# Routing of a mixture of experts: an eight-highest search, shares in one step, a weight load in six pieces

## The chip, the cores and the metric

The kernel runs on one core of a Trainium2 chip. The metric is the device time of one execution in microseconds (us); lower is better.

## The reference

`x` is 32 sequences of 128 tokens with 128 features. Four blocks follow one another, each added to `x` and each behind a LayerNorm: a 16-head cross attention to a context of 77 tokens followed by a self attention and a feed-forward part; a mixture of 8 experts with two experts per token and a shared expert beside them; a two-way cross attention with a gate; a mixture in which each expert picks its 33 tokens of a sequence. The change lies in the second block:

```python
xn = xf * rsqrt(mean(xf * xf) + eps)                # xf: 4096 tokens
probs = softmax(xn @ router_w.T)                    # 8 experts
topk_p, topk_i = top_k(probs, 2)                    # ties: the lower expert first
rw = topk_p / sum(topk_p)                           # the two shares of a token
# the first 640 tokens of each expert, in token order, are dispatched
eout = (silu(xg @ rg) * (xg @ ru)) @ rd             # routed experts
shared = (silu(x @ sg) * (x @ su)) @ sd             # shared expert
return shared + routed
```

## The kernel before

**Tiling.** The 32 sequences are 8 groups of `GB` = 4. Tokens of a sequence lie on the 128 partitions. Attention is worked off in 16 units (`UNITS`): the cross attention (`c`) and self attention (`s`) of each group; self attention of groups 0 to 7 is unit 4, 6, 8, 10, 12, 13, 14, 15 (`SPOS`).

**Order.** Every engine runs the same loop over beats `n` from -11 to 159, written out by hand in `sp`, `pe`, `dve`, `act` and `pool`. Unit `i` starts at beat `8 i`; a step is placed by `d = n - 8 i`. Within a beat each engine has a fixed order of its steps and waits on semaphores. So a late step of one engine holds what is queued behind it there. The score maxima of a unit, eight beats of PE matmuls (L603), DVE reductions (L1196), ACT exponentials (L1665) and value products (L636), are the fabric. From beat 118 on the shared expert's matmuls (`shared`, L781, L782, L790) are woven in: 2, then 7/3 of them a beat. Each passes from PE to ACT (tanh, L1720) to DVE (L1350, L1354), and PE may take a bank again when DVE is done with it. Behind the loop the routed experts run, then the third and fourth blocks.

**Routing, on DVE**, for the group `g` of a self attention unit:
- `logits` (`d` = 30, L1260) writes eight logits for each of the 4 sequences.
- `choose` (`d` = 31, last in its beat but for LayerNorms). It compares every logit with every other (256 elements per token), adds a tie rule, sums to a rank, and takes rank 0 and rank 1 as `RR`. `SEL` is their sum; the scan L1293 makes the running count along the group and raises `v_sel`.
- `margin` (`d` = 32, L1300 to L1307): the difference of the two logits, `DEN`. ACT takes its exponential at `d` = 33 (L1794).
- `cum` on PE (`d` = 35 for groups 0 to 2, 33 for the others, L769, L770) waits for `v_sel` and sums over the tokens.
- `counts` and `places` (one and two beats behind `cum`) give the place of each token. POOL writes the tokens out with them (`scatter`, L2027).
- `shares` (`d` = 41 for groups 0 to 3, 37 for the others, L1335 to L1342): `w0 = 1 / (1 + DEN)`, `w1 = DEN w0`, and zero where the place is over capacity. `combine` reads them long after, in the third block.

**Spreads and loads, on SP.** In beats `d` = -16 to -12 of a unit SP spreads its queries and keys over partitions (`spread_k` L443, `spread_q` L447, a mask L436 or L438). PE's scores of that unit start at `d` = -11 and wait for all of them. At `d` = -1 SP sends the row of maxima (L489). The shared expert's weights `Wc`, 128 rows of 12 KB, are one load at beat 40 (L533), behind the first keys of unit 7:

```python
if n == 40:
    e.dma_start(Wc, A["pc"][:, 0:3072]).then_inc(d_wc, 16)
```

PE needs them from beat 118 on.

Of the kernel before, what the change touches and what calls it, by code (L numbers as in the profile page):

```python
# [9 lines left out]
I32 = mybir.dt.int32  # L10
U32 = mybir.dt.uint32
ALU = mybir.AluOpType
# [11 lines left out]
C_ID, C_LT, C_AT, C_IO, C_TR, C_EB, C_EC, C_MK, C_N = 0, 128, 256, 384, 417, 481, 489, 497, 537  # L24


def constants():
# [12 lines left out]
    c[:, C_TR:C_TR + 64] = (np.arange(8)[None, :] < np.arange(8)[:, None]).reshape(-1)  # L40
# [157 lines left out]
def program(nc, A, out, cst):  # L198
    ctx = ExitStack()
    with ctx:  # L200
# [61 lines left out]
        RR, RP, M2, IDF = r(128, 2, GB, 8), r(128, 2, GB, 8), r(128, 2, GB), r(128, 2, GB)  # L262
        DEN = r(128, GB)
        CMP, CM2 = r(128, GB, 8, 8), r(128, GB, 8, 8)
# [149 lines left out]
        def sp(e):  # L414
# [69 lines left out]
            for n in range(BEAT0, BEAT1):  # L484
# [47 lines left out]
                if n == 40:  # L532
                    e.dma_start(Wc, A["pc"][:, 0:3072]).then_inc(d_wc, 16)  # L533
# [53 lines left out]
        def pe(e):  # L587
# [186 lines left out]
            def shared(k):  # L774
                (hw, c), B = SHSEQ[k], bank_of(k)
                if c < 8:
                    xt = XLT[:, 256 * hw:256 * hw + 256]
                    L.wait_ge(a_t2, hw // 2 + 1)
                    L.wait_ge(d_wc, 16)
# [360 lines left out]
        def dve(e):  # L1140
# [128 lines left out]
            def choose(g):  # L1269

                Lg = grp(LG, g)
                other = Lg.unsqueeze(2).to_broadcast([128, GB, 8, 8])
                own = Lg.unsqueeze(3).to_broadcast([128, GB, 8, 8])
                tri = CST[:, C_TR:C_TR + 64].unsqueeze(1).to_broadcast([128, GB, 64])
                c1, c2 = (a.rearrange("p b e f -> p b (e f)") for a in (CMP, CM2))
# [20 lines left out]
            def margin(g):  # L1296

                R, P = rr()
# [19 lines left out]
            def places(g):  # L1318
# [5 lines left out]
                L.tick(e.tensor_reduce(IDF, RP, AX, ALU.add))  # L1324
                L.own_done()
                e.tensor_copy(IDX.bitcast(I32)[:, :, gb], IDF).then_inc(v_idx, 1)
                L.tick(e.tensor_scalar(M2, IDF, float(E1 * CAP1), None, ALU.min))
# [3 lines left out]
            def shares(g):  # L1331
                gb = slice(GB * g, GB * g + GB)
                w0, w1_ = WT[:, 0, gb], WT[:, 1, gb]
                L.wait_ge(a_ex, g + 1)
# [7 lines left out]
                L.tick(e.tensor_tensor(WT[:, :, gb], WT[:, :, gb], IDF, ALU.mult))  # L1342
# [17 lines left out]
            for n in range(BEAT0, BEAT1):  # L1360
# [142 lines left out]
            def r_top(u):  # L1503
                sm, sco = SM[u % 2], SCO[u]
                smb = sm.unsqueeze(2).to_broadcast([128, 8, 8])
                L.wait_ge(a_ex, NG + u + 1)
# [670 lines left out]
```

## Time and profile before

| | us |
|---|---|
| three runs | 1137.52, 1141.02 (median), 1141.60 |
| profiled execution, its own time | 1140.32 |
| its span in the profile | 1138.5 |
| PE busy | 989.6 |
| DVE busy | 676.0 |
| ACT busy | 590.1 |
| POOL busy | 468.6 |
| mean granted clock of PE | 0.928 of full |

How to read it: the span is what the trace covers, 1.8 us less than the execution's own time. PE's matmuls are pipelined, so its busy time overstates it somewhat. Busy times are averages over stages: the attention stage lies from 0 to about 440 us, attention's end together with the shared expert to 614, the routed experts to about 730, the last two blocks behind. A row of the timeline reads: start, duration, engine, line, operation, tiles and shapes, count, and in square brackets the idle time of the engine ahead of it with what ended it. A tile called `arena` is any of many in one large buffer. `issue` stands where nothing that the profile shows was waited for.

### The profile page before, as it was taken

To read this page: it belongs to the slowest core of one execution; us is meant where nothing else is said; L and a number is where in the kernel's file an instruction comes from. 1 tells how busy PE (TensorE), PEld (TensorE's weight loads), DVE (VectorE), ACT (ScalarE), POOL (GpSimd) and SP (SyncE) were. 2 spreads that over 40 slices of the span, in tenths; PEclk is the share of its full clock that TensorE was granted. 3 is DMA by queue.
4 is the path that set the end of the run, shared out by engine and by line. 5 is a ranking of instruction groups with operands and counts; after the bars stand their busy time and mean duration, and the time that the engine had idled before them with its cause. 6 is when DMAs were issued, how large, how long until landed. Compare 5 with 4: busy or idle time off the path is not lost.

```text
span 1138.5 us, 23362 instructions
## 1 busy us (share of the span) xinstructions
PE 989.6 (87%) x8694; PEld 771.1 (68%) x8694; DVE 676.0 (59%) x2162; ACT 590.1 (52%) x1350; POOL 468.6 (41%) x752
## 2 busy tenths in 40 slices
PE   4888888797888878978998999988887897898998
PEld 2666555566565656767787888766776686787877
DVE  4556664767676777557684333366788458366241
ACT  4667668686766767633333333223432644645553
POOL 5245544646657574575552000222554335213010
PEclk8788888889788989989999999989998999998999
DMA  7644442222322212000001333300000241330511
GB/s 182 167 133 126 113 123 71 67 71 58 90 66 77 72 41 80 11 12 8 6 4 37 103 102 90 114 15 12 20 22 14 64 118 27 70 94 19 149 57 56
DMA packets 72224, 78.58 MB, mean 69 GB/s; under 512 B 8389, under 2 KB 64052, under 8 KB 71984
## 3 DMA queue, kind: packets, MB, share of 16 engines
q1 hardware_dynamic: 66384, 69.61, 21.9%
q0 software_dynamic: 4096, 6.84, 2.8%
q8 instruction: 70, 1.15, 0.4%
q10 hardware_dynamic: 1632, 0.64, 0.3%
q14 instruction: 42, 0.34, 0.1%
HBM read 38.25 MB, written 11.68 MB: 44 GB/s over the span
## 4 chain that ended last, share of the span: by engine, by line
PE 50%; DVE 19%; POOL 11%; ACT 10%; issue 6%; DMA 2%; SPq 1%; DVEq 0%; POOLq 0%; ACTq 0%
PE pb L1060 5%; PE pb L1050 4%; PE pb L790 4%; PE pb L887 3%; PE pb L874 3%; PE pb L876 3%; PE pb L747 3%; PE pb L636 2%; DVE arena L1196 2%; POOL arena L1950 2%; DVE XB L1158 2%; PE pb L781 2%; PE pb L782 2%; DVE arena L1354 2%; DVE arena L1350 2%
## 5 line engine op out<-in xcount | busy, mean ns | idle before, releaser
L1196 DVE TENSOR_REDUCE arena<-pb 128x4 f32<-128x308 f32 (+1 forms) x256 | 136.2, 575 | 74.5 <-PE pb L603 74.3
L1665 ACT ACTIVATE arena<-pb 77x512 f32<-77x512 f32 (+1 forms) x256 | 138.8, 598 | 58.2 <-PE pb L619 57.6
L2106 POOL DMA_INDIRECT arena<-yd,arena x64 | 63.6, 994 | 140.3 <-issue 140.3
L1720 ACT ACTIVATE arena<-pb 128x256 f32<-128x256 f32 x128 | 48.9, 384 | 128.9 <-PE pb L782 123.1
L1948 POOL TENSOR_SCALAR arena<-arena 128x4 f32<-128x4 f32 x48 | 10.0, 208 | 227.4 <-DVE arena L1151 226.0
L636 PE MATMUL pb<-arena 77*32 77x128 f32 (+1 forms) x2048 | 93.5, 307 | 0.0
L781 PE MATMUL pb<-XLT,arena 128*128 128x256 f32 x256 | 78.2, 387 | 2.1 <-DVE arena L1354 2.1
L603 PEld LDWEIGHTS pb<-arena 64*128 64x128 bf16 x1024 | 30.9, 104 | 68.4 <-issue 32.2
L782 PE MATMUL pb<-XLT,arena 128*128 128x256 f32 x256 | 77.1, 383 | 0.0
L2027 POOL DMA_INDIRECT xd<-XB,arena x64 | 64.1, 1002 | 29.6 <-issue 19.6
L1886 ACT ACTIVATE arena<-pb,arena 128x264 f32<-128x264 f32 x128 | 54.6, 484 | 40.7 <-PE pb L1050 40.6
L1350 DVE SCALAR_TENSOR_TENSOR arena<-arena,pb 128x256 f32<-128x256 f32 x128 | 53.1, 415 | 32.2 <-ACT arena L1720 32.1
L1050 PE MATMUL pb<-arena 128*128 128x264 f32 x256 | 64.8, 389 | 7.4 <-ACT arena L1886 7.4
L619 PE MATMUL pb<-arena 64*77 64x128 bf16 (+1 forms) x1024 | 58.5, 240 | 14.3 <-ACT arena L1665 10.8
L603 PE MATMUL pb<-arena 64*128 64x77 bf16 (+1 forms) x1024 | 51.7, 229 | 21.1 <-DVE arena L1196 13.9
L658 PE MATMUL pb<-CST,XB 128*128 128x128 f32 x192 | 37.3, 328 | 37.1 <-DVE XB L1158 18.1
L2002 POOL TENSOR_TENSOR arena<-arena 128x512 f32<-128x512 f32 (+1 forms) x32 | 34.0, 1062 | 79.6 <-ACT arena L1681 79.6
L636 PEld LDWEIGHTS pb<-arena 77*32 77x32 f32 (+1 forms) x2048 | 54.0, 119 | 15.8 <-issue 5.1
L1060 PE MATMUL pb<-arena 128*128 128x264 f32 x256 | 62.5, 387 | 1.8 <-DVE arena L1564 1.8
L790 PEld LDWEIGHTS pb<-arena 128*128 128x128 f32 x512 | 59.3, 192 | 6.9 <-DVE arena L1354 5.4
L790 PE MATMUL pb<-arena 128*128 128x128 f32 x512 | 60.4, 276 | 3.6 <-DVE arena L1354 3.6
L1432 DVE TENSOR_TENSOR arena<-pb,arena 128x320 f32<-128x320 f32 x64 | 31.5, 492 | 46.2 <-ACT arena L1846 46.2
(232 smaller groups left out, 2445.1 us busy)
## 6 DMA issues: line engine op xcount, KB each, us to landing
arena<-arena SPq DMA_DIRECT2D x190, 128.0 KB, 2.5
arena<-in_pe SPq DMA_DIRECT2D x32, 514.5 KB, 3.6
arena<-in_pr SPq DMA_DIRECT2D x8, 768.0 KB, 5.0
arena<-arena SPq DMA_DIRECT2D x43, 77.0 KB, 2.4
xd<-arena SPq DMA_DIRECT2D x8, 320.0 KB, 3.5
arena<-xd SPq DMA_DIRECT2D x8, 320.0 KB, 5.6
yd<-arena SPq DMA_DIRECT2D x8, 320.0 KB, 5.1
XO<-in_x SPq DMA_DIRECT2D x8, 256.0 KB, 3.7
```

The source lines that it names most:

```text
L603: ins = e.matmul(bk[B + h2][:, nk * t:nk * t + nk], q_s[a, 4 * h + t, 128 * b:128 * b + 128], k_s[a, 4 * h + t, b * nk:b * nk + nk], start ...
L636: ins = e.matmul(bk[4][32 * k:32 * k + 32, 128 * q:128 * q + 128], va[0:nk, h9:h9 + 32], PT[n % 2][0:nk, 512 * h2 + 128 * t:512 * h2 + 128 ...
L781: e.matmul(bk[B][:, 0:256], sg[:, 128 * c:128 * c + 128], xt, start=True, stop=True)
L782: e.matmul(bk[B][:, 256:512], su[:, 128 * c:128 * c + 128], xt, start=True, stop=True) \
L790: ins = e.matmul(bat(bk[B], b), SH[(8 * hw + c) % NSI][:, 128 * b:128 * b + 128], sd[:, c, :], start=(c == 0), stop=(c == 7))
L1050: e.matmul(bk[c][:, 0:N8], EWP[q % 4][:, 128 * c:128 * c + 128], XE[:, k, :], start=True, stop=True).then_inc(p_e1, 1)
L1060: ins = e.matmul(bk[4][:, 0:N8], w2e[:, c, :], HEP[q % 2][:, c, :], start=(c == 0), stop=(c == 3))
L1196: e.tensor_reduce(NM[i % 2][0][:, b, 4 * h:4 * h + 4, h2], bk[B + h2][:, 0:4 * nk].rearrange("p (t k) -> p t k", t=4), AX, ALU.max, negate ...
L1350: L.tick(e.scalar_tensor_tensor(si, si, 1.0, bk[B][:, 0:256], ALU.add, ALU.mult))
L1665: e.activation(PT[n % 2][0:nk, 512 * hf:512 * hf + 512], bk[2 + hf][0:nk, :], ACT.Exp, scale=SC8).then_inc(a_exp, 1)
L2027: e.indirect_dma_start(xd, bass.IndirectOffsetOnAxis(ap=IDX.bitcast(U32)[:, k, x:x + 1], axis=0), XB[:, x, :], None, bounds_check=E1 * CAP ...
L2106: e.indirect_dma_start(G[x % 8], None, yd, bass.IndirectOffsetOnAxis(ap=IDG.bitcast(U32)[:, k, b:b + 1], axis=0), bounds_check=None, oob_i ...
```

## The change

It has three parts.

1. **`choose` is computed in another way and split.** A MAX8 per sequence gives the eight highest logits in order. Two comparisons mark where the logits equal the highest and the second. A scan counts marked experts along each row of eight, so that of equal logits the lower comes first; where first and second are equal, the second mark's count is lowered by one. The new `select`, at `d` = 32 ahead of `margin`, takes the marks whose count is 1, then forms `SEL` and the running count as before. So `v_sel` is raised in beat 32, not 31. `margin` keeps the copy alone.
2. **Shares once.** `DEN` and `IDF` hold all 32 sequences. `choose` writes the difference of the two highest, ACT takes one exponential of 32 columns at `d` = 33 of the last group, and `shares` runs once, at `d` = 37 of the last group.
3. **The shared weights** are six loads of 512 columns (2 KB a row, 256 KB in all) at beats 44, 52, 60, 68, 76 and 84. PE waits for all six.

```diff
-                if n == 40:
-                    e.dma_start(Wc, A["pc"][:, 0:3072]).then_inc(d_wc, 16)
+                if n in range(44, 92, 8):
+                    w = slice(512 * ((n - 44) // 8), 512 * ((n - 44) // 8) + 512)
+                    e.dma_start(Wc[:, w], A["pc"][:, w]).then_inc(d_wc, 16)
...
             def choose(g):
...
-                L.tick(e.tensor_tensor(CM2, other, own, ALU.is_equal))
-                L.tick(e.tensor_tensor(CMP, other, own, ALU.is_gt))
-                L.own_done()
-                L.tick(e.tensor_tensor(c2, c2, tri, ALU.mult))
-                L.own_done()
-                L.tick(e.tensor_tensor(c1, c1, c2, ALU.add))
-                L.own_done()
-                L.tick(e.tensor_reduce(f2(PRE), CMP.rearrange("p b e f -> p (b e) f"), AX, ALU.add))
-                L.own_done()
-                L.tick(e.tensor_scalar(RR[:, 0], PRE, 0.0, None, ALU.is_equal))
-                L.tick(e.tensor_scalar(RR[:, 1], PRE, 1.0, None, ALU.is_equal))
+                for b in range(GB):
+                    L.tick(e.max(TOP[:, b, :], Lg[:, b, :]))
+                L.own_done()
+                for k in range(2):
+                    L.tick(e.tensor_tensor(RP[:, k], Lg, top[:, k].unsqueeze(2).to_broadcast([128, GB, 8]), ALU.is_equal))
+                L.tick(e.tensor_tensor(M2[:, 0], top[:, 0], top[:, 1], ALU.is_equal))
+                L.tick(e.tensor_tensor(DEN[:, GB * g:GB * g + GB], top[:, 1], top[:, 0], ALU.subtract))
+                L.own_done()
+                L.tick(e.tensor_tensor_scan(seen, CST[:, C_M8:C_M8 + 64], cand, 0.0, ALU.mult, ALU.add))
+                L.own_done()
+                L.tick(e.tensor_tensor(k4[:, 1], k4[:, 1], M2[:, 0].unsqueeze(2).to_broadcast([128, GB, 8]), ALU.subtract))
+                L.own_done()
+
+            def select(g):
...
+                L.tick(e.scalar_tensor_tensor(RR.rearrange("p k b e -> p (k b e)"), seen, 1.0, cand, ALU.is_equal, ALU.mult))
                 L.own_done()
                 if g:
                     L.wait_ge(p_cum, g)
...
             def margin(g):
...
-                L.tick(e.tensor_tensor(P, both(grp(LG, g)), R, ALU.mult))
-                L.tick(e.tensor_copy(SELX[:, :, 0], CUM[:, :, GB]))
-                L.own_done()
-                L.tick(e.tensor_reduce(M2, RP, AX, ALU.add))
-                L.own_done()
-                if g:
-                    L.wait_ge(a_ex, g)
-                e.tensor_tensor(DEN, M2[:, 1], M2[:, 0], ALU.subtract).then_inc(v_ex, 1)
+                ins = e.tensor_copy(SELX[:, :, 0], CUM[:, :, GB])
...
-                        if d == (41 if g < 4 else 37):
-                            shares(g)
+                        if g == NG - 1 and d == 37:
+                            shares()
...
                         if d == 32:
+                            select(g)
                             margin(g)
...
-                        if d == 33:
-                            L.wait_ge(v_ex, g + 1)
+                        if g == NG - 1 and d == 33:
+                            L.wait_ge(v_ex, 1)
                             e.activation(DEN, DEN, ACT.Exp).then_inc(a_ex, 1)
```

How this moves DVE's instructions around `choose` and `margin` of group 6. Before (names ahead of `<-` are what is written; `x2` means twice in a row):

```order
L1277 TENSOR_TENSOR arena<-arena 128x256
L1278 TENSOR_TENSOR arena<-arena 128x256
L1280 TENSOR_TENSOR arena<-arena,CST 128x256
L1282 TENSOR_TENSOR arena<-arena 128x256
L1284 TENSOR_REDUCE arena<-arena 128x32
L1286 TENSOR_SCALAR arena<-arena 128x32
L1287 TENSOR_SCALAR arena<-arena 128x32
L1291 TENSOR_TENSOR arena<-arena 128x4x8
L1293 SCALAR_TENSOR_TENSOR arena<-CST,arena 128x40
L1148 BN_STATS arena<-XB 128x6 x4
L1151 BN_AGGR arena<-arena 128x2 x4
```

With the change (line numbers are those of the changed kernel):

```order
L1279 MAX arena<-arena 128x8 x4
L1282 TENSOR_TENSOR arena<-arena 128x32 x2
L1283 TENSOR_TENSOR arena<-arena 128x4
L1284 TENSOR_TENSOR arena<-arena 128x4
L1286 SCALAR_TENSOR_TENSOR arena<-CST,arena 128x64
L1288 TENSOR_TENSOR arena<-arena 128x32
L1149 BN_STATS arena<-XB 128x6 x4
L1152 BN_AGGR arena<-arena 128x2 x4
L1353 SCALAR_TENSOR_TENSOR arena<-arena,pb 128x256
L1357 SCALAR_TENSOR_TENSOR arena<-arena,pb 128x256
L1361 TENSOR_TENSOR XO<-pb,XO 128x256
L1294 SCALAR_TENSOR_TENSOR arena<-arena 128x64
```

The five passes over 256 elements are gone. `SEL` and the running count no longer stand ahead of the LayerNorm (BN_STATS) but behind it and behind a shared step, where `margin` was; L1294 is `select`'s first.

SP's queue around the load, before:

```order
L443 DMA arena<-arena 16x8x308 x3
L417 DMA XO<-in_x 128x4x128
L533 DMA arena<-in_pc 128x3072
L447 DMA arena<-arena 16x8x512 x3
L443 DMA arena<-arena 16x8x308 x2
L447 DMA arena<-arena 16x8x512 x2
L443 DMA arena<-arena 16x8x308
L436 DMA arena<-msk 16x8x308
L447 DMA arena<-arena 16x8x512
L489 DMA arena<-arena 16x8x512
```

With the change:

```order
L443 DMA arena<-arena 16x8x308 x3
L417 DMA XO<-in_x 128x4x128
L447 DMA arena<-arena 16x8x512 x3
L443 DMA arena<-arena 16x8x308 x2
L447 DMA arena<-arena 16x8x512 x2
L443 DMA arena<-arena 16x8x308
L436 DMA arena<-msk 16x8x308
L447 DMA arena<-arena 16x8x512
L534 DMA arena<-in_pc 128x512
L489 DMA arena<-arena 16x8x512
```

The load stood ahead of ten of the round's transfers; its first sixth now stands behind the last of them. The other five pieces stand at the same place of the next five rounds.

## Rows read from the trace of the kernel before

**Rows 1.** which engines hold the chain of waits that ended last (the page)
```profile
PE 50%; DVE 19%; POOL 11%; ACT 10%; issue 6%; DMA 2%; SPq 1%; DVEq 0%; POOLq 0%; ACTq 0%
```

**Rows 2.** DMA issues by kind: tiles, queue, count, KB each, median us to landing
```profile
arena<-arena SPq DMA_DIRECT2D x190, 128.0 KB, 2.5
...
arena<-in_pc SPq DMA_DIRECT2D x1, 1536.0 KB, 10.4
```

**Rows 3.** windows: us, busy of PE, PEld, DVE, ACT, POOL, clock, DMA share, GB/s
```profile
160.00:165.00 5.00, 2.80 (x52) 2.04 (x53) 4.79 (x16) 2.58 (x6) 3.37 (x4) 1.00 1.00 242
165.00:170.00 5.00, 4.14 (x59) 2.82 (x59) 3.50 (x14) 2.21 (x5) 3.37 (x7) 0.65 0.15 41
```

**Rows 4.** timeline of PE, 165 to 168 us: start, duration, operation, idle before
```profile
165.28 0.27 PE L619 MATMUL pb<-arena 64*77 64x128 bf16 x3 [1.93 <-issue]
...
167.90 0.44 PE L603 MATMUL pb<-arena 64*128 64x77 bf16 x8 [0.58 <-DMA arena<-arena]
```

**Rows 5.** timeline of SP's queue
```profile
162.52 1.75 SPq L447 DMA_DIRECT2D arena<-arena  x1
```

**Rows 6.** timeline of DVE, `choose` of group 6
```profile
559.24 0.42 DVE L1277 TENSOR_TENSOR arena<-arena 128x256 f32<-128x256 f32 x1
...
562.10 0.85 DVE L1148 BATCH_NORM_STATS2 arena<-XB 128x6 f32<-128x128 f32 x4
562.98 0.38 DVE L1151 BATCH_NORM_AGGREGATE arena<-arena 128x2 f32<-128x6 f32 x4
```

**Rows 7.** groups by line, DVE: count, busy us, mean ns, idle before
```profile
L1522 DVE MAX8 arena<-arena 64x8 f32<-64x128 f32 x20 | 5.7, 285 | 0.6
```

**Rows 8.** timeline of DVE, `choose` of group 1
```profile
289.99 1.26 DVE L1277 TENSOR_TENSOR arena<-arena 128x256 f32<-128x256 f32 x1
...
295.12 0.27 DVE L1248 TENSOR_TENSOR XB<-pb,XB 128x128 f32<-128x128 f32 x1
```

**Rows 9.** timeline of POOL beside it
```profile
289.70 1.27 POOL L1997 TENSOR_TENSOR XB<-XB,rows 128x512 f32<-128x512 f32 x1
```

**Rows 10.** timeline of PE: its gaps behind the edited places
```profile
296.02 0.93 PE L658 MATMUL pb<-CST,XB 128*128 128x128 f32 x4 [3.13 <-DVE arena L1241]
...
416.56 0.63 PE L658 MATMUL pb<-CST,XB 128*128 128x128 f32 x4 [0.63 <-DVE arena L1241]
...
453.11 1.98 PE L739 MATMUL pb<-XLT,arena 128*128 128x512 f32 x4 [1.03 <-DVE arena L1241]
...
503.26 1.11 PE L658 MATMUL pb<-CST,XB 128*128 128x128 f32 x4 [5.75 <-ACT XB L1655]
...
516.44 1.83 PE L747 MATMUL pb<-arena 128*128 128x128 f32 x14 [2.48 <-DVE arena L1260]
...
539.77 2.50 PE L790 MATMUL pb<-arena 128*128 128x128 f32 x20 [0.45 <-DVE arena L1354]
...
549.84 3.84 PE L747 MATMUL pb<-arena 128*128 128x128 f32 x32 [1.46 <-DVE arena L1260]
...
573.30 3.84 PE L790 MATMUL pb<-arena 128*128 128x128 f32 x32 [1.61 <-DVE arena L1354]
```

**Rows 11.** timeline of POOL behind `choose` of group 6
```profile
563.46 0.20 POOL L1948 TENSOR_SCALAR arena<-arena 128x4 f32<-128x4 f32 x1 [8.58 <-DVE arena L1151]
```

**Rows 12.** timeline of DVE, `shares` of groups 3 and 5
```profile
450.10 1.02 DVE L1340 TENSOR_TENSOR arena<-arena 128x4 f32<-128x4 f32 x1
...
548.83 0.16 DVE L1335 TENSOR_SCALAR arena<-arena 128x4 f32<-128x4 f32 x1
...
549.59 0.19 DVE L1260 TENSOR_TENSOR arena<-pb,arena 128x32 f32<-128x32 f32 x1
```

**Rows 13.** timeline of DVE, `margin` of group 7 and what follows
```profile
591.07 0.22 DVE L1300 TENSOR_TENSOR arena<-arena 128x64 f32<-128x64 f32 x1
...
591.74 0.41 DVE L1350 SCALAR_TENSOR_TENSOR arena<-arena,pb 128x256 f32<-128x256 f32 x1
```

**Rows 14.** timeline of PE, `cum` of group 7
```profile
591.38 0.31 PE L769 MATMUL pb<-arena,CST 128*128 128x32 f32 x2
```

More of the change, by code:

```diff
@@ L39, in constants @@
     c[:, C_IO:C_IO + CAP2] = np.arange(1, CAP2 + 1)
-    c[:, C_TR:C_TR + 64] = (np.arange(8)[None, :] < np.arange(8)[:, None]).reshape(-1)
+    c[:, C_M8:C_M8 + 64] = np.arange(64) % 8 > 0
     c[:, C_EB:C_EB + 8] = np.arange(8) * (CAP1 // 128)
@@ L261, in program @@
         VAL, PRE = (r(128, GB, 8) for _ in range(2))
-        RR, RP, M2, IDF = r(128, 2, GB, 8), r(128, 2, GB, 8), r(128, 2, GB), r(128, 2, GB)
-        DEN = r(128, GB)
-        CMP, CM2 = r(128, GB, 8, 8), r(128, GB, 8, 8)
+        RR, RP, M2, IDF = r(128, 2, GB, 8), r(128, 2, GB, 8), r(128, 2, GB), r(128, 2, NB)
+        DEN = r(128, NB)
+        CMP, TOP, PADS = r(128, GB, 8, 8), r(128, GB, 8), r(128, 160)
         PT = [r(128, 1024) for _ in range(2)]
@@ L1271, in choose @@
                 Lg = grp(LG, g)
[L1272 to L1275, printed above, removed]
+                cand, seen = RP.rearrange("p k b e -> p (k b e)"), CMP[:, 0].rearrange("p e f -> p (e f)")
+                top = TOP[:, :, 0:2].rearrange("p b k -> p k b")
+                k4 = seen.rearrange("p (k b e) -> p k b e", k=2, b=GB)
                 L.wait_ge(v_lg, g + 1)
-                L.tick(e.tensor_tensor(CM2, other, own, ALU.is_equal))
-                L.tick(e.tensor_tensor(CMP, other, own, ALU.is_gt))
+                for b in range(GB):
+                    L.tick(e.max(TOP[:, b, :], Lg[:, b, :]))
                 L.own_done()
-                L.tick(e.tensor_tensor(c2, c2, tri, ALU.mult))
+                for k in range(2):
+                    L.tick(e.tensor_tensor(RP[:, k], Lg, top[:, k].unsqueeze(2).to_broadcast([128, GB, 8]), ALU.is_equal))
+                L.tick(e.tensor_tensor(M2[:, 0], top[:, 0], top[:, 1], ALU.is_equal))
+                L.tick(e.tensor_tensor(DEN[:, GB * g:GB * g + GB], top[:, 1], top[:, 0], ALU.subtract))
                 L.own_done()
-                L.tick(e.tensor_tensor(c1, c1, c2, ALU.add))
+                L.tick(e.tensor_tensor_scan(seen, CST[:, C_M8:C_M8 + 64], cand, 0.0, ALU.mult, ALU.add))
                 L.own_done()
-                L.tick(e.tensor_reduce(f2(PRE), CMP.rearrange("p b e f -> p (b e) f"), AX, ALU.add))
+                L.tick(e.tensor_tensor(k4[:, 1], k4[:, 1], M2[:, 0].unsqueeze(2).to_broadcast([128, GB, 8]), ALU.subtract))
                 L.own_done()
-                L.tick(e.tensor_scalar(RR[:, 0], PRE, 0.0, None, ALU.is_equal))
-                L.tick(e.tensor_scalar(RR[:, 1], PRE, 1.0, None, ALU.is_equal))
+            def select(g):
+                cand, seen = RP.rearrange("p k b e -> p (k b e)"), CMP[:, 0].rearrange("p e f -> p (e f)")
+                L.tick(e.scalar_tensor_tensor(RR.rearrange("p k b e -> p (k b e)"), seen, 1.0, cand, ALU.is_equal, ALU.mult))
                 L.own_done()
@@ L1296, in margin @@
             def margin(g):
-                R, P = rr()
                 L.wait_ge(v_sel, g + 1)
-                L.tick(e.tensor_tensor(P, both(grp(LG, g)), R, ALU.mult))
-                L.tick(e.tensor_copy(SELX[:, :, 0], CUM[:, :, GB]))
-                L.own_done()
-                L.tick(e.tensor_reduce(M2, RP, AX, ALU.add))
-                L.own_done()
-                if g:
-                    L.wait_ge(a_ex, g)
-                e.tensor_tensor(DEN, M2[:, 1], M2[:, 0], ALU.subtract).then_inc(v_ex, 1)
+                ins = e.tensor_copy(SELX[:, :, 0], CUM[:, :, GB])
+                if g < NG - 1:
+                    L.tick(ins)
+                else:
+                    ins.then_inc(v_ex, 1)
             def counts(g):
@@ L1323, in places, with shares @@
                 L.own_done()
-                L.tick(e.tensor_reduce(IDF, RP, AX, ALU.add))
+                L.tick(e.tensor_reduce(IDF[:, :, gb], RP, AX, ALU.add))
                 L.own_done()
-                e.tensor_copy(IDX.bitcast(I32)[:, :, gb], IDF).then_inc(v_idx, 1)
-                L.tick(e.tensor_scalar(M2, IDF, float(E1 * CAP1), None, ALU.min))
+                e.tensor_copy(IDX.bitcast(I32)[:, :, gb], IDF[:, :, gb]).then_inc(v_idx, 1)
+                L.tick(e.tensor_scalar(M2, IDF[:, :, gb], float(E1 * CAP1), None, ALU.min))
                 L.own_done()
                 e.tensor_copy(IDG.bitcast(I32)[:, :, gb], M2).then_inc(v_idg, 1)
[L1331 to L1334, printed above, removed]
+            def shares():
+                w0, w1_ = WT[:, 0, :], WT[:, 1, :]
+                L.wait_ge(a_ex, 1)
                 L.tick(e.tensor_scalar(w1_, DEN, 1.0, None, ALU.add))
```

10 lines of the change are left out of this document (5 added, 5 removed).

## The prediction

> **What bounds the kernel now.** I read the chain of waits first. PE holds half of the chain that ended last, DVE 19%, POOL 11% [rows 1]. So an instruction saved on DVE is worth time only where PE stands idle behind it, and nowhere more than that idle time. The change touches the routing of the first mixture of experts (`choose`, `margin`, `shares`) and one load, so I looked at three kinds of place: the load, PE's gaps around each `choose` and `shares`, and the one spot where the running count is now ready later.
>
> **The load.** The 1.5 MB of shared weights took 10.4 us to land, where a typical spread of queries or keys takes 2.5 [rows 2]. While it ran, the DMA engines were busy for all of 160 to 165 us [rows 3]. PE stopped twice in that stretch: 1.93 us with no releaser, which I read as waiting for its own instructions, and 0.58 us for a spread (L447) that gates the scores of the next unit. That scores group (L603) began at 167.90 [rows 4]. The spread was issued at 162.52 [rows 5]; at the usual 2.5 us it lands at 165.0 to 165.3, and PE's work before the scores, without the stall, ends there too. Gain: 167.9 - 165.3 = **2.6 us**. PE's granted clock was full until 165 and 0.65 in the next 5 us, a mix of its two levels (1.2 and 2.4 GHz) [rows 3]. 5 x 0.35 = 1.75 us of work at the full clock was lost there; without the stops I take **1.2** back, so **3.8** in all. The ends are 0, if the six pieces cost as much as they save, and 4.4.
>
> The six pieces stand in the order right behind the last spread of a round and ahead of a max row (L489) that is due three beats later. A piece should take a sixth of 10.4, 1.7 us. I cost them at nothing. The cover is that no spread is due for three beats; if it is gone, see the rival below.
>
> **`choose`.** In group 6 it takes from 559.24 to 562.10 before the next instruction starts: 2.86 us, most of it five passes over 256 elements [rows 6]. The new one has four MAX8 on 8 elements, two comparisons on 32, two operations on 4, a scan over 64, one subtraction. None of the four MAX8 waits for another. Four such small instructions in a row (BN_AGGR) took 0.38 us [rows 6]; the other bound is MAX8 on 128 elements at 285 ns, four times, 1.14 [rows 7]. I take 0.38, since the nearest in size decides. Four tensor operations without waits between them: 0.45, at the same pitch plus a last one of 0.22. The scan 0.30 and the subtraction 0.25, somewhat over the 0.22 of a pass over 64 elements [rows 13], the waits between steps within. Sum 1.4, I take 1.55 us: **1.3 saved** (0.6 with the other bound).
>
> The page "VectorE: DVE Perf Modes", section on the TRN2 errata, of the Trainium skill says that the fixed term of an instruction is about 150 cycles whatever its size. By an estimate from it ten instructions in series cost about 1.8 us, so that each `choose` would save 1.05 instead of 1.3, and the total would fall by about 1 us. Four instructions in 0.38 us, 0.1 each, speak for less than that rule where none waits for another [rows 6].
>
> Where does the saving reach PE?
> - Group 1 (L1277 at 289.99): it lasts until 295.12, 5.1 us, since L1277 ran 1.26 us [rows 8] beside POOL's L1997 [rows 9] and others were stretched too. PE waited 3.13 us behind it for L1241 [rows 10]. New: MAX8 until 290.4, comparisons held until POOL is done at 290.97, end at about 292.4. **2.7** of the gap close. PE's matmuls behind the gap ran slowly: the four of L658 took 0.93 us there and 0.63 at 416.56 [rows 10]. A warm clock gives back about **1.2** over that group and the next ones (ends 0 and 1.5).
> - Group 3: PE's gap is 0.63 [rows 10]: **0.6**.
> - Group 4: the next thing is a LayerNorm, then POOL, and PE waits 5.75 us until 503.26 [rows 10]: the whole **1.3**.
> - Group 5: the gap behind it is 0.45 [rows 10]: **0.4**.
> - Group 6: L1148, then POOL, which had stood idle 8.58 us for it [rows 11], then a gap of 1.61 [rows 10]: **1.3**.
> - Groups 0, 2 and 7: PE has no gap: 0. What hides them is PE's own work.
>
> Sum for `choose`: 2.7 + 1.2 + 0.6 + 1.3 + 0.4 + 1.3 = **7.5**.
>
> **`shares`.** Seven of eight go. One without obstruction takes 548.83 to 549.59, 0.76 us [rows 12]; in groups 0 to 3 L1340, four elements, took about 1.0 us instead of 0.16 beside POOL's long operations; one such row stands in [rows 12]. Group 3: 3.4 us leave DVE, the gap is 1.03: **1.0**. Group 4 (gap 2.48) and group 5 (gap 1.46): 0.7 each, **1.4** [rows 10]. In groups 0 to 2 the chain of waits runs through a row of POOL operations that were ready before DVE was done: nothing, although DVE loses nearly 2 us each. Group 6: PE has no gap. The single `shares` at the end works on 32 and 64 elements in place of 4 and 8: -0.1. Sum **2.3**.
>
> **`select` and `margin`.** A pass over 64, one over 32, a scan and a copy, 0.85 us, replace a `margin` of 0.67 (591.07 to 591.74) [rows 13]. The running count is thus ready one beat later. For groups 0 to 6 PE's `cum` comes later still. For group 7 it does not: PE ran L769 at 591.38 [rows 14], and DVE reaches `select` no sooner than 591.07, where `margin` began [rows 13], because the shared step ahead of it waits for ACT; the scan ends at about 591.8. PE then has no idle time to give: **-0.4**. Behind PE there are the shared experts' matmuls, which wait with it.
>
> **ACT** loses seven small exponentials and, by the order, two of its table loads; a later one now stands at group 7. PE's gaps name ACT nowhere near them: 0.
>
> **Sum:** 3.8 + 7.5 + 2.3 - 0.4 = 13.2 us. I keep back 1 us, since closed gaps expose what is late next (groups 1 and 3 stand in the attention stage, where ACT and POOL are nearly as busy as DVE). 1140.3 us of the profiled execution (span 1138.5, 1.8 around it) less 12.2 is **1128 us**. The profiled execution lies 0.7 below the median of the three runs, 1141.0. About 0.5%, 5.7 us, is what a measurement of this kernel can tell from no change.
>
> **Rivals.**
> - *The slack is absorbed.* POOL chains take over as in groups 1 and 2 of `shares`, so that only the direct parts pay: 2.6 for the load, 2.7 for group 1: 5.3 less, **1135**. For it: 11% of the chain is POOL. Against: POOL stood idle before group 6. Chance 0.18.
> - *The port.* The page "SBUF — State Buffer" of the Trainium skill, section on who interferes with whom, says that a DVE instruction with two SBUF inputs and a POOL instruction that reads SBUF lock each other out for their whole length. As a mechanism of this kernel: every new comparison and scan can be held by one POOL operation, as L1277 was at 289.99, by up to 1.27 us [rows 8, 9]. The traces agree that such holds exist. Once per `choose` in the five groups that pay would cancel 5 x 1.27 = 6.4: **1134**. Against: in groups 4 to 6 POOL stands idle while `choose` runs [rows 11]. Chance 0.10.
> - *More clock.* PE stays at the full clock for longer stretches before 300 us; the two clock terms of 1.2 become 8 together, as if all the low-clock stretches like the one of [rows 3] behind the edited places went: **1122**. Chance 0.12.
> - *The pieces collide* (slower). Each piece sits directly behind L447, on whose landing the scores of the next beat wait. If a piece costs 1.7 us of landing and a stop like the 1.93 us one, that is 3.6, six times 21.8, against the other gains of 9.4: **1153**. It decides from 1.6 us per piece. For it: the two stops at 165 [rows 4]. Against: a piece moves a sixth. Chance 0.04.
> - *The change does not do what it says.* The order shows one `shares` and six loads; I give it nothing.
>
> **Chances.** My case 0.56. Faster by over 0.5% (below 1135.3): my case, the clock, most of the port, half of the absorbed: 0.56 + 0.12 + 0.06 + 0.08 = 0.82. Same: 0.14. Slower: 0.04. My case alone spans 1123 to 1133: the lower bounds of the load (0) and of `choose` (0.6 in place of 1.3, three groups) on one side, the upper ones on the other. The range for 8 in 10 takes in the absorbed case and half of the clock's: **1119 to 1137**.
>
> **What would show it.** DVE busy falls from 676 to about 650 us. `choose` lasts 1.4 to 1.8 us. The row of the load shows six at about 3 us to landing, and the PE stop of 1.93 us near 163 is gone. The gap of 3.13 us near 293 shrinks below 1, the one of 5.75 to about 4.4. PE waits about 0.4 us for the scan at its last `cum`. I am wrong if the gaps stay and name POOL or ACT instead, or if L603 waits for DMA in more rounds.

## The result and the profile after

The changed kernel took 1124.95 us in the median of four runs (1122.17 to 1126.75), the kernel before 1139.37 (1137.52 to 1141.6). The ratio is 0.9871, with a 95% interval of 0.984 to 0.9901: 14.4 us less. On another chip, with more runs, the same two kernels stood at 1128.46 and 1137.23, ratio 0.9914 (0.9884 to 0.9945), which is 9.8 us. The mean of both ratios is 0.989, or 12.2 us. I had forecast 12.2; with intervals of 3 us and more around each ratio, that the two agree so closely is chance. All ratios leave out three slow executions (1167.77 and 1576.70 us of the kernel before, 1840.52 of the kernel before with the single `shares`).

The profiled execution took 1125.38 us, with a span of 1123.6. Its page: busy time by engine, the engines in the chain of waits that ended last, and the row of the load.

```profile
PE 982.7 (87%) x8694; PEld 769.2 (68%) x8694; DVE 653.2 (58%) x2135; ACT 585.7 (52%) x1341; POOL 467.4 (42%) x752
...
PE 54%; DVE 16%; POOL 11%; ACT 10%; issue 6%; DMA 2%; SPq 1%; DVEq 0%; POOLq 0%; ACTq 0%
...
arena<-in_pc SPq DMA_DIRECT2D x6, 256.0 KB, 3.0
```

DVE is busy 23 us less than before (676.0) and has 16% of the chain instead of 19% [rows 1]. A sixth of the load lands in 3.0 us. The new `choose` of group 6 in DVE's timeline, up to the layer-norm statistics:

```profile
544.88 0.37 DVE L1279 MAX8 arena<-arena 128x8 f32<-128x8 f32 x4
545.28 0.30 DVE L1282 TENSOR_TENSOR arena<-arena 128x32 f32<-128x32 f32 x2
545.49 0.16 DVE L1283 TENSOR_TENSOR arena<-arena 128x4 f32<-128x4 f32 x1
545.57 0.16 DVE L1284 TENSOR_TENSOR arena<-arena 128x4 f32<-128x4 f32 x1
545.76 0.29 DVE L1286 TENSOR_TENSOR_SCAN arena<-CST,arena 128x64 f32<-128x64 f32 x1
546.09 0.19 DVE L1288 TENSOR_TENSOR arena<-arena 128x32 f32<-128x32 f32 x1
546.31 0.87 DVE L1149 BATCH_NORM_STATS2 arena<-XB 128x6 f32<-128x128 f32 x4
```

It takes 1.43 us (546.31 - 544.88) where the old one took 2.86 [rows 6]. Four independent MAX8 share 0.37 us. PE's gaps behind the last four groups, in its timeline of the changed kernel:

```profile
492.22 0.66 PE L659 MATMUL pb<-CST,XB 128*128 128x128 f32 x4 [4.33 <-ACT XB L1659]
...
504.10 2.16 PE L748 MATMUL pb<-arena 128*128 128x128 f32 x17 [1.72 <-DVE arena L1261]
...
535.47 3.84 PE L748 MATMUL pb<-arena 128*128 128x128 f32 x32 [0.69 <-DVE arena L1261]
...
557.55 3.84 PE L791 MATMUL pb<-arena 128*128 128x128 f32 x32 [1.61 <-DVE arena L1357]
...
576.11 0.42 PE L770 MATMUL pb<-arena,CST 128*128 128x32 f32 x2 [0.32 <-DVE arena L1300]
...
592.44 3.84 PE L791 MATMUL pb<-arena 128*128 128x128 f32 x32 [0.81 <-DVE arena L1357]
```

Against [rows 10]: 5.75 became 4.33 (`choose` of group 4), 2.48 became 1.72 and 1.46 became 0.69 (`shares` of groups 4 and 5), and 0.32 is new (the running count of group 7, one beat later). The 1.61 stands, but a gap of 1.27 at L781 ahead of it shrank to 0.15.

**How the traces are compared.** PE runs one group of 16 matmuls of L636 (L637 with the new load) in each of 128 beats, 0 to 127. The time between two of them is the length of a stretch, in any of the kernels. Behind beat 127, PE's later instructions are measured from the group of beat 127. A single pair of profiles misleads here. Beats 0 to 38 hold nothing that any kernel here edits, yet they took from 103.9 to 110.6 us in the 14 profiles. The difference goes with the granted clock: over these beats its mean was 0.82 to 0.84 in the three longest and 0.89 in the shortest. Two windows of the same work, first of the kernel before, then of the changed one (the clock is the third number from the end):

```profile
50.00:60.00 10.00, 9.45 (x151) 6.52 (x152) 4.93 (x13) 6.79 (x15) 0.77 (x1) 0.83 0.73 199
```
```profile
50.00:60.00 10.00, 10.00 (x112) 6.89 (x108) 3.86 (x10) 5.70 (x12) 0.77 (x1) 0.52 0.55 159
```

PE was at half its clock (1.2 of 2.4 GHz) for nearly all of that window in the changed kernel, and was about 2 us behind at beat 38, where no edit stands ahead. So I read each place from all profiles that have the same code there.

### The profile page after: what moved, and what is told of

Read it like the earlier page. It is cut to its first block, busy times and chain, and to the rows that moved or that the text cites. A ratio compares the mean times of both kernels' runs of the same rounds, so it can differ in the third digit from the quotient of the medians.

```text
span 1123.6 us, 23339 instructions
## 1 busy us (share of the span) xinstructions
PE 982.7 (87%) x8694; PEld 769.2 (68%) x8694; DVE 653.2 (58%) x2135; ACT 585.7 (52%) x1341; POOL 467.4 (42%) x752
## 4 chain that ended last, share of the span: by engine, by line
PE 54%; DVE 16%; POOL 11%; ACT 10%; issue 6%; DMA 2%; SPq 1%; DVEq 0%; POOLq 0%; ACTq 0%
PE pb L1061 5%; PE pb L791 4%; PE pb L1051 4%; PE pb L888 3%; PE pb L637 3%; PE pb L875 3%; PE pb L877 3%; PE pb L748 3%; PE pb L782 3%; PE pb L783 3%; DVE arena L1197 2%; DVE XB L1159 2%; POOL arena L1954 2%; DVE arena L1149 2%; PE pb L740 2%
## 5 line engine op out<-in xcount | busy, mean ns | idle before, releaser
L637 PE MATMUL pb<-arena 77*32 77x128 f32 (+1 forms) x2048 | 92.6, 305 | 0.0
L791 PEld LDWEIGHTS pb<-arena 128*128 128x128 f32 x512 | 59.6, 193 | 6.5 <-DVE arena L1357 5.0
L637 PEld LDWEIGHTS pb<-arena 77*32 77x32 f32 (+1 forms) x2048 | 53.4, 118 | 14.7 <-issue 3.4
L1051 PEld LDWEIGHTS pb<-arena 128*128 128x128 f32 x256 | 47.2, 190 | 17.0 <-issue 7.0
```

The source lines that it names most:

```text
L637: ins = e.matmul(bk[4][32 * k:32 * k + 32, 128 * q:128 * q + 128], va[0:nk, h9:h9 + 32], PT[n % 2][0:nk, 512 * h2 + 128 * t:512 * h2 + 128 ...
L791: ins = e.matmul(bat(bk[B], b), SH[(8 * hw + c) % NSI][:, 128 * b:128 * b + 128], sd[:, c, :], start=(c == 0), stop=(c == 7))
L1051: e.matmul(bk[c][:, 0:N8], EWP[q % 4][:, 128 * c:128 * c + 128], XE[:, k, :], start=True, stop=True).then_inc(p_e1, 1)
```

## The experiments

Twelve kernels in three groups of four; each group ran on a chip of its own (first, second, third below, in the order of the table). Ratios are to the kernel before on the same chip.

| kernel | median us | before | ratio (95%) |
|---|---|---|---|
| changed, one load at beat 40 | 1126.66 | 1137.06 | 0.9913 (0.989 to 0.9937) |
| before + six loads | 1135.15 | 1137.06 | 0.9975 (0.9957 to 0.9993) |
| changed, shares per group | 1129.34 | 1137.06 | 0.9933 (0.991 to 0.9956) |
| before + single shares | 1139.39 | 1137.06 | 1.0018 (1.0 to 1.0035) |
| changed, again | 1128.46 | 1137.23 | 0.9914 (0.9884 to 0.9945) |
| before, old choose later in its beat | 1137.67 | 1137.23 | 0.9993 (0.9972 to 1.0014) |
| changed, pad in groups 1, 3 to 6 | 1130.22 | 1137.23 | 0.9941 (0.9918 to 0.9963) |
| changed, three moves | 1125.58 | 1137.23 | 0.9869 (0.9829 to 0.9908) |
| changed, pad in groups 0, 2, 7 | 1148.62 | 1156.05 | 0.9936 (0.9903 to 0.9969) |
| changed, one load at beat 44 | 1151.26 | 1156.05 | 0.9937 (0.9903 to 0.997) |
| changed, two tail moves | 1146.87 | 1156.05 | 0.9888 (0.9828 to 0.9948) |
| before + new choose only | 1155.72 | 1156.05 | 0.9993 (0.9958 to 1.0028) |

Lengths of stretches, us, in the profiles from the first two of these chips and of the two kernels themselves (a kernel whose pad, see below, stands in the stretch is left out of its row):

| beats | what stands there | old code | new code |
|---|---|---|---|
| 38 to 48 | the load | 30.67, 30.77, 31.52, 32.15 | 27.67, 27.97, 28.73, 29.22, 29.23, 29.34 |
| 62 to 72 | choose 0 | 37.42, 38.02, 38.69, 39.04 | 35.18, 35.21, 36.01, 36.02, 37.20, 37.87 |
| 76 to 84 | choose 1 | 31.31, 31.61, 32.95, 33.94 | 29.87, 30.03, 31.60, 33.15, 33.28 |
| 95 to 101 | choose 2 | 23.19, 25.00, 27.70, 27.70 | 23.27, 24.03, 24.05, 24.06, 24.07, 24.07 |
| 111 to 117 | choose 3 | 22.36, 23.98, 24.00, 24.04 | 20.90, 20.90, 20.91, 20.93, 21.08 |
| 105 to 111 | shares 2 | 22.86, 22.86, 23.05, 23.07 | 22.70, 22.88, 23.03, 23.04, 23.05, 23.16 |
| 121 to 127 | shares 3 | 34.65, 34.67, 34.68, 34.69 | 33.57, 33.57, 33.58, 33.58, 33.58, 33.63 |

### The load

Changed kernel with the old load:

```
-                if n in range(44, 92, 8):
-                    w = slice(512 * ((n - 44) // 8), ...)
-                    e.dma_start(Wc[:, w], A["pc"][:, w])...
+                if n == 40:
+                    e.dma_start(Wc, A["pc"][:, 0:3072]).then_inc(d_wc, 16)
```

> The changed kernel with the shared weights again in one load of 1.5 MB, at beat 40; choose, select and the single shares stay new. Theory A (my account: the single load made PE stop and wait, and six pieces cost nothing): 2.6 to 3.8 us slower than the changed kernel, about 1128 to 1129 us, with the PE stop near 160 us and the L604 wait for DMA back. Theory B (the two traces: the same stretch gained 3.0 us over beats 43 and 44, and 1.6 came back in beat 45 for another wait and the clock): 1.0 to 1.9 us slower, about 1126.5. Theory C (the pieces cost what they save): within 0.7 us of the changed kernel.

PE's timeline at the load, SP's queue, and the row of the load, in this kernel:

```profile
164.22 0.44 PE L603 MATMUL pb<-arena 64*128 64x77 bf16 x8 [3.65 <-DMA arena<-arena]
...
151.04 0.56 SPq L533 DMA_DIRECT2D arena<-in_pc  x1
151.65 1.94 SPq L447 DMA_DIRECT2D arena<-arena  x3
...
arena<-in_pc SPq DMA_DIRECT2D x1, 1536.0 KB, 9.5
```

The wait is back. It is one wait of 3.65 us for the spread, where the profile of before had 1.93 "issue" and 0.58 "DMA" [rows 4]; the kernel with old load and single shares shows 3.84, the one with only the new `choose` 3.70. The old `choose` moved later shows the split again, 1.66 "issue" and 0.84 "DMA"; what the "issue" part waited for stays open. The whole run (1126.66) could not be told from the changed kernel's on the next chip (ratios 0.9913 and 0.9914).

The kernel before with only the six loads:

> The kernel before with only the six loads. Theory A: 1135.6 to 1136.8 us against 1139.4. Theory B: about 1138. Theory C: 1139 to 1140. If the pieces were what collides (the slower rival), over 1141.

1.9 us less by the medians, 2.8 by the ratio, at least 0.8: between A and B, and against the slower rival. By stretches, on the mean over all eight kernels with six loads and all five with one at beat 40, the third chip's too: beats 38 to 48 take 2.9 us less with six (2.6 by the table's profiles alone). The wait of 2.5 to 3.8 us is gone, and one of 1.9 to 2.0 us in beat 45 for DVE (L1242), which no kernel with the load at 40 has, stands in its place. Beats 48 to 62 take 0.8 us more. Most of that is 1.0 us in beat 51 of four of the eight, where the granted clock was 0.50 or 0.51 and not 0.64. Net 2.1.

Is it the size or the place? The load again in one, four beats later:

```
-                if n in range(44, 92, 8):
...
+                if n == 44:
+                    e.dma_start(Wc, A["pc"][:, 0:3072]).then_inc(d_wc, 16)
```

> The changed kernel with one load of 1.5 MB, issued at beat 44, where the first of the six pieces stands, instead of beat 40. Theory A (size: a spread of the next beats waits behind a long load wherever it stands): PE waits 2 to 4 us for a spread about four beats later than with the load at beat 40, beats 38 to 48 take 31 us, or the stretch behind them is that much longer, as against 28.7 with six loads; 2 to 3 us slower than the changed kernel. Theory B (place: behind the last spread of a round nothing is due): as fast as the changed kernel, beats 38 to 48 in 28.7 us.

SP's queue, PE's timeline and the row of the load in this kernel:

```profile
156.41 0.59 SPq L533 DMA_DIRECT2D arena<-in_pc  x1
...
161.66 0.47 PE L720 MATMUL pb<-CST,arena 128*128 128x128 f32 x1 [1.88 <-DVE arena L1241]
...
arena<-in_pc SPq DMA_DIRECT2D x1, 1536.0 KB, 6.6
```

Beats 38 to 48 take 28.78 us, as with six loads, and no PE matmul waits for a transfer there. The 1.5 MB land in 6.6 us, not 9.5, with no spreads beside them. Theory B holds in the profile: the place behind the last spread does it, and cutting the load up adds nothing that the profile shows. The ratios on this chip (0.9937 against 0.9936 and 0.9888 of two kernels with six loads) are too wide to add to that.

### Shares

The changed kernel with `shares(g)` and its exponential per group, on slices of `DEN` and `IDF`:

```
-                        if g == NG - 1 and d == 37:
-                            shares()
+                        if d == (41 if g < 4 else 37):
+                            shares(g)
...
-                        if g == NG - 1 and d == 33:
+                        if d == 33:
```

> The changed kernel with shares and its exponential again once per group (beat 41 or 37 of each, as before); choose, select and the six loads stay new. Theory A (my terms: only groups 3, 4 and 5 pay, 1.0 + 0.7 + 0.7, and the single one costs 0.1): 2.3 us slower than the changed kernel, about 1127.3. Theory B (the traces: the beats behind shares of groups 1 and 2 each became 2 us shorter, which I had put at nothing, while the single shares costs PE 0.8): 4 to 6 us slower, about 1130. Theory C (what groups 1 and 2 gained came back within four beats): 1 to 2.5 slower, so not to be told from A by the time alone, but by the beats.

And the kernel before with only the single `shares` (the reverse of this edit, in its old `margin`):

> The kernel before with only the shares made once for all groups (the old choose, margin and load). Theory A: 2.3 us faster than before, 1137.1. Theory B: 4 to 6 faster, about 1134.5. If the parts add up, the changed kernel's 14.4 us less the load's and the shares' part is what choose and select are worth: 7.1 by my account, and the gain here and the loss in the run with shares per group are the same number.

Alone the single `shares` is worth nothing: 1139.39 against 1137.06, and the interval excludes the 2.3 us of Theory A as well as Theory B. Yet its places gain what A said: beats 121 to 127 became 1.1 us shorter, and behind groups 4 and 5 PE's gaps 0.76 and 0.77 shorter; in groups 1 and 2 the whole stretch is unchanged, since what beats 89 and 105 save (2.1 and 2.0 us) returns in the next four, where PE waits 3.05 us for ACT, in one wait (L1659 in the changed kernel). What ate the rest in this profile is the clock. This kernel's PE, its timeline at the gap of group 4 and the window behind:

```profile
514.39 3.79 PE L747 MATMUL pb<-arena 128*128 128x128 f32 x18 [1.72 <-DVE arena L1260]
...
515.00:520.00 5.00, 5.00 (x33) 4.96 (x33) 0.22 (x1) 0.00 (x0) 4.16 (x5) 0.74 0.04 14
```

The clock fell behind that gap (0.74 in this window, 1.00 at the same place in the kernel before), and PE lost 1.5 us. Over the 14 profiles such a fall stands behind this gap in 3 of the 5 with `shares` per group, where the gap is 2.48 us long (shares per group, old choose later, new choose only), and in 1 of the 9 with the single `shares`, where it is 1.72: this one. The changed kernel with shares per group is about 2 us slower by the ratios (0.9933 against 0.9914, on two chips and with overlapping intervals), as Theories A and C said; this fall is the difference that the profiles show beside the gaps. A single `shares` also costs at its own place: PE waits 0.81 us where it waited 0.54, since it lasts 1.3 us, not 0.76.

### Choose

Does DVE time count where it is spent? Four passes for nothing behind the new `choose`:

```
+                if g in (1, 3, 4, 5, 6):
+                    for _ in range(4):
+                        L.tick(e.tensor_tensor(CMP[:, 1:4]..., CST[:, 0:192], CST[:, 128:320], ALU.add))
+                        L.own_done()
```

> The changed kernel with four more passes over 192 elements (about 1.5 us, work for nothing) behind the new choose of groups 1, 3, 4, 5 and 6. This gives back the DVE time that the new choose saved there. Theory A (my sum): the 7.5 us of choose come back, less the clock's 1.2: 5.5 to 7.5 us slower than the changed kernel. Theory B (the traces: only groups 4, 5 and 6 pay, 1.4 + 1.25 + 1.1 us, and group 3; the rest was the phase of the clock): 4 to 5 us slower, the late ones to be seen one by one. Theory C (slack absorbs it): under 3.

DVE in group 6 and PE behind group 4 in this kernel:

```profile
551.15 1.53 DVE L1294 TENSOR_TENSOR arena<-CST 128x192 f32<-128x192 f32 x4
...
494.61 1.11 PE L659 MATMUL pb<-CST,XB 128*128 128x128 f32 x4 [5.77 <-ACT XB L1666]
```

The gap of 5.75 is back, as 5.77. Counted from beat 127 to the last running count, PE gained 5.6 us in the changed kernel and 0.1 with the pad; group 3's stretch took 22.02 instead of 20.9. So 6.6 us came back in the profile. From beat 127 to the end its profile is 5.7 us longer than that of the changed kernel on the same chip (653.2 and 647.5 us), so nothing is won back there. The whole run lost 1.8 us by the medians and 3.1 by the ratios. Theory A fits the places, C the medians; the two ratios' intervals overlap. The two profiled executions differ by 4.1 us the other way up to beat 127 (439.9 against 443.9 us), by the clock; whether the rest went that way in the other runs stays open.

The same pad where the prediction put nothing, `g in (0, 2, 7)`:

> The changed kernel with the same four passes over 192 elements (1.5 us) behind the new choose of groups 0, 2 and 7, where the prediction gave the change nothing since PE showed no gap behind choose there. Theory A (the prediction): 0 to 0.5 us slower than the changed kernel. Theory B (three profiles of kernels with the old choose show PE's L658 waiting 1.2 to 2.4 us behind DVE at group 2, which the one profile before did not show; group 0 has a shorter stretch too): 1 to 3 us slower, most of it at group 2 (beats 95 to 101, 24.1 us in the changed kernel), and nothing at group 7.

Group 2's stretch took 27.35 us against 27.0 to 27.2 in the other three on this chip, group 0's 37.58 against 35.6 to 37.5, group 7 nothing (the count waits 1.17 us, like two of its neighbours). The ratio (0.9936) lies within the others' intervals. By the lengths Theory A fits. But the gap that B names is back at group 2; PE's timeline in this kernel:

```profile
351.51 0.63 PE L659 MATMUL pb<-CST,XB 128*128 128x128 f32 x4 [1.56 <-DVE arena L1242]
```

No other kernel with the new `choose` has it. It made beat 95 longer by 1.3 us (4.29 against 2.92 to 2.98). Beats 96 to 100 were 1.0 to 1.2 us shorter than in the other three: on this chip PE waits 2.1 us in beat 98 for ACT where it waits 0.8 on the others, and the stretch is 3 us longer in every kernel. So the prediction's "no gap" is wrong for group 2, and what the gap costs depends on what PE waits for next.

At group 0 nothing came back, and nothing had been won. The table's 2.0 us there go with the clock: 1.1 of them lie in beat 62, which took 4.97 and 5.06 us with the old `choose`, 5.01 to 5.06 with the new one and 5.04 with the pad wherever the granted clock was 0.51 or 0.52, and 2.76 us where it was full. Beat 63 took 2.6 us in all 14 profiles. Most of the other 0.9 lies in beats 66 and 67, where the granted clock of two profiles with the old `choose` was lower still.

The old `choose` with its place changed, nothing else: issued behind the beat's layer-norm statistics.

```
-                        if d == 31:
-                            choose(g)
                 for i in range(NU):
...
+                for i in range(NU):
+                    ...
+                    if kind == "s" and d == 31:
+                        choose(g)
```

> The kernel before with one move and no other edit: its old choose, with all its passes over 256 elements, is issued behind the layer-norm statistics of the same beat instead of ahead of them. That alters three places, the beats of groups 4, 5 and 6, where the next group's statistics, then POOL, then PE wait for it. Theory A (a DVE instruction costs only where PE's next work stands behind it): PE's gap of 5.75 us behind group 4 shrinks by 2.9, and groups 5 and 6 give 1.2 to 2 each: 5 to 7 us faster than before, about 0.995. Theory B (the saved DVE time as such is what counts): no change, 0.999 to 1.001.

PE's timeline in this kernel:

```profile
502.60 1.11 PE L658 MATMUL pb<-CST,XB 128*128 128x128 f32 x4 [4.00 <-ACT XB L1657]
...
515.18 5.02 PE L747 MATMUL pb<-arena 128*128 128x128 f32 x28 [2.48 <-DVE arena L1260]
...
535.00 1.13 PE L739 MATMUL pb<-XLT,arena 128*128 128x512 f32 x2 [0.41 <-DVE arena L1316]
```

Neither theory: the gap of group 4 shrank by 1.75 us, not 2.9, since POOL, between the statistics and PE, now waits for the step behind the moved `choose` (L1158), as its timeline shows:

```profile
490.07 1.29 POOL L1997 TENSOR_TENSOR XB<-XB,rows 128x512 f32<-128x512 f32 x1 [0.93 <-DVE XB L1158]
```

Group 5 gave 0.1, since PE there waits for L1316 (`counts`), which the moved passes still stand ahead of; group 6 gave 0.9. Behind the 2.48 and behind the next gap, 1.46, the clock fell, which cost 1.5 and 1.6 us. Moving the long `choose` is no substitute for a short one.

The new `choose` alone:

> Only the new choose and select: one load at beat 40, shares and exponential per group as before. From the prediction's terms: 7.5 - 0.4 = 7.1 us faster than before, ratio 0.9938. From the segments of the ten profiles so far (beats 62 to 127 take 256.7 us with the old choose and 248.7 with the new one and the single shares, of which 1.1 is shares of group 3; behind beat 127 choose gives 4.1 and select takes 0.5): 10 us faster, ratio 0.991. By the product of the parts run so far (0.9933 over 0.9975): 0.9958.

0.9993, at most 4.9 us faster: below all three expectations, though the interval takes in the product of the parts. This chip was 19 us slower with the kernel before, and every kernel there shows a stop of ACT that none shows on the other chips. ACT's timeline, the two tail moves' kernel:

```profile
414.47 0.60 ACT L1681 ACTIVATE arena<-pb 128x512 f32<-128x512 f32 x1 [3.92 <-remote]
```

PE waits 4.0 us behind it in beats 111 to 117 (28 us instead of 21), just where `choose` of group 3 pays on the other chips. The profile does not say what "remote" is. So the new `choose` has no clean measurement alone. From the ratios 0.9933 and 0.9975 I estimate it at 0.4%, 4.8 us, with shares per group, give or take 3 us by their intervals.

### The repeat, and a faster version

> The changed kernel once more, with more runs, on the chip of its neighbours here. The first comparison gave a ratio of 0.9871. The four runs that leave out or do one part alone gave 0.9975 (six loads alone), 1.0018 (shares alone), 0.9913 (all but the six loads) and 0.9933 (all but the single shares). If the parts add up, the first and the third give 0.989 and the second and the fourth 0.995. Theory A (the parts add up; single profiles differ by the phase of PE's granted clock): 0.988 to 0.991. Theory B (the parts help each other): 0.987 or less.

0.9914 is at Theory A's end, the first comparison at B's. Both intervals hold 0.989.

Three moves in the changed kernel: `choose` behind the layer-norm loop, `select` of group 7 right behind its `choose`, and

```
-                        if g == NG - 1 and d == 37:
-                            shares()
...
             for k in range(shared_before(BEAT1 - 1), shared_before(BEAT1)):
                 shared(k)
+            shares()
```

> The changed kernel with three moves: choose behind the layer-norm statistics of its beat (groups 4, 5 and 6), the select of group 7 one beat earlier (31, as before), and the single shares behind the last beat, where DVE waits 3.6 us for the experts. Theory A: 1.4 + 1.2 + 1.1 us for choose as far as PE's gaps allow, 0.5 for select and 0.8 for shares (PE's gaps of 0.32 and 0.81 us go): 3 to 5 us faster than the changed kernel, ratio 0.983 to 0.986 to before. Theory B: the gaps are taken over by POOL and ACT, and it is within 1.5 us of the changed kernel.

PE's timeline and two windows of it:

```profile
561.44 3.84 PE L791 MATMUL pb<-arena 128*128 128x128 f32 x32 [1.44 <-DVE arena L1357]
...
601.97 0.74 PE L864 MATMUL pb<-CST,arena 128*128 128x128 f32 x5 [1.47 <-DVE arena L1357]
...
602.00:605.00 3.00, 2.15 (x8) 1.51 (x9) 0.79 (x4) 2.05 (x3) 0.00 (x0) 0.78 0.28 85
605.00:608.00 3.00, 3.00 (x8) 1.92 (x8) 0.49 (x1) 0.73 (x2) 0.00 (x0) 0.65 0.08 24
```

The gaps of 0.32 and 0.81 are gone and group 4's is 3.56. From beat 127 to the experts' first transposes PE takes 2.0 us less than in the changed kernel. Behind the 1.47 the clock then fell (0.78 and 0.65 in the two windows), and eight us later 1.7 of the 2.0 were gone. The median is 2.9 us below the changed kernel's on the same chip, the ratio 0.9869 against 0.9914, 5.1 us: at or near Theory A. It is the fastest on its chip, though its interval overlaps the changed kernel's.

The two tail moves alone:

> The changed kernel with two of the three moves of the all-moved run: select of group 7 at beat 31, and the single shares behind the last beat. Choose stands where it stood. Theory A: PE's gaps of 0.32 us (cum of group 7) and 0.81 us (behind the single shares) go, and from the end of beat 127 to the experts' first transposes the kernel takes 1.3 to 2 us less than the changed one; ratio to before lower by 0.001 to 0.002. Theory B: the gap moves to the experts' start and the time stays.

0.9888, the lowest ratio on its chip, with a wide interval. PE's gap at `cum` of group 7 is gone (1.25 in the kernel with one load at 44), and so is the one behind `shares`. The experts' first transposes stand 1.9 us sooner behind beat 127 (124.1 us against 126.0), the second ones 0.2 (133.9 against 134.1). So Theory A holds up to the experts and B behind them: the clock falls behind the gap of 1.47 in both kernels with the tail moves, and in none of the other twelve.

## Why the prediction was right, and where it was not

The total, 12.2 us against 14.4 and 9.8 measured, came out right. Its terms did not all.

- **The load**: 2.6 us direct is right in size (2.6 to 2.9 in beats 38 to 48), as a longer wait gone less a new one for DVE in beat 45. The 1.2 us of clock were wrong: the next fourteen beats gave 0.8 back. Net 2.1 instead of 3.8. My reason, a spread behind the load, is right; that the pieces matter is not.
- **`choose` lasts** 1.43 us; I took 1.55. The Trainium skill's page "VectorE: DVE Perf Modes", section on the TRN2 errata, led to 1.8 by an estimate. The trace has 0.37 us for four MAX8 that do not wait for each other, so a fixed term for each in series is too much here. In group 1, beside POOL's operations, it lasts 1.9 us.
- **Group 1**, 3.9 us with its clock, was mis-sized: about 0.9 by stretches (32.45 on the mean against 31.59). Beat 79 alone, where its gap stands, took 7.36, 3.97, 2.85 and 2.61 us with the old `choose` and 2.6 with the new one on the same chips, pad or not. I read 5.1 us for `choose` and a gap of 3.13 as typical. They were one execution's meeting of two timelines. DVE and POOL of the kernel before:

```profile
293.00 1.66 DVE L1286 TENSOR_SCALAR arena<-arena 128x32 f32<-128x32 f32 x1
...
293.44 1.18 POOL L2002 TENSOR_TENSOR arena<-arena 128x512 f32<-128x512 f32 x1
```

In the other three profiles with this code POOL's operation came later, L1286 ran 0.43 us, and PE's gap was 0 to 1.33.

- **Groups 2 and 3**, priced 0 and 0.6, gave about 2.0 and 2.6 on the mean; group 2 gave nothing in the profile of before and 3.7 in two others. "PE has no gap: 0" was read from the same execution, in which PE came late to group 2 because of a wait of 3.23 us earlier. Group 0's price of 0 stands. In the kernel with only the single shares PE shows:

```profile
353.27 0.65 PE L658 MATMUL pb<-CST,XB 128*128 128x128 f32 x4 [2.37 <-DVE arena L1241]
...
414.19 0.63 PE L658 MATMUL pb<-CST,XB 128*128 128x128 f32 x4 [1.15 <-DVE arena L1241]
```

The first is group 2, the second group 3; neither is left with the new `choose`. That the failing terms nearly cancel (3.0 too high at group 1, 4.0 too low at groups 2 and 3, 1.7 too high at the load, 1.4 too low behind beat 127) is luck.

- **Groups 4, 5, 6** behaved as worked out where the clock was full: 1.41 (1.3), 1.25 (0.4) and 1.1 (1.3). In group 5 I missed a second gap, of 0.51 us at L739, which the same saving closed.
- **`shares`**: 1.1, 0.76 and 0.77 at the three places, as forecast (1.0, 0.7, 0.7), and nothing in groups 0 to 2. The whole run does not show the sum. The single one lasts 1.3 us and costs PE 0.3, not 0.1.
- **`select`** of group 7: PE lost 0.48 (0.4).
- **The port rival.** DVE is held beside POOL in the changed kernel too. POOL, then DVE, at group 1:

```profile
292.57 1.15 POOL L2006 TENSOR_TENSOR arena<-arena 128x512 f32<-128x512 f32 x1 [1.88 <-ACT arena L1685]
```
```profile
292.63 1.16 DVE L1298 TENSOR_TENSOR arena<-arena 128x32 f32<-128x32 f32 x1
```

L1298 takes 0.21 to 0.29 us in the other groups. By the Trainium skill's page "SBUF — State Buffer", section on who interferes with whom, a DVE instruction with two SBUF inputs, as L1298 is, and a POOL instruction that reads SBUF lock each other out; the trace agrees, with 1.16 us. But `select` is short and PE had other work: no gap followed. The hold is real, its price of 6.4 us was not.

The load, groups 1, 2 and 3, the `shares` of group 3 and the way from beat 127 to the experts (128.35 us before, 123.0 changed) sum to 2.1 + 0.9 + 2.0 + 2.6 + 1.1 + 5.3 = 14 us, some 2 more than the whole runs. The falls of the clock behind the remaining gaps, different in each execution, are the likely rest; no run isolates them.

The span of my case, 1123 to 1133, did not follow from its bounds either: added up, the ones named give about 1126 (with the 1 us that I kept back) to 1134, and the 1124.95 of the first comparison lies outside that, though inside the range for 8 in 10.

## What to carry to other kernels

Where the clock moves between levels, one profile shows one meeting of the timelines; a gap, or the lack of one, behind a periodic step should be read over all its repeats and from a second profile before it is priced. When a large load stalls a pipeline, first look at what is queued behind it: moving it past the last due transfer did as much here as cutting it up. A step that nobody waits for belongs behind the one that somebody does, but only if nothing else waits behind it.

## What the runs showed of the hardware

- The same 38 beats took 103.9 to 110.6 us in 14 executions, the granted clock falling at different moments. Behind group 4's gap of 3.6 to 5.8 us it fell in all 14; behind gaps of 1.4 to 2.5 us only in some (behind the same 1.47 us in 2), at a cost of 1.5 to 1.7 us each where it could be read.
- One load of 1.5 MB took 9.5 to 10.4 us to land beside spreads (five profiles), and 6.6 without them (one).
- Four MAX8 on 8 elements that do not wait for each other took 0.34 to 0.37 us together.
- The third chip ran the kernel before in 1156 us, the others in 1137 to 1139, with stops of ACT of 3.2 to 4.6 us, and of DVE of up to 7.2, that the profile puts down to "remote". None of the ten profiles from the other chips has such a stop of over 1.5 us.
